# Causal attention with the negated maxima turned as 64 rows of one bank and placed by eight transfers, and another order at a layer's end

## The reference, cut to what matters

```python
scores = einsum('blhd,bmhd->bhlm', q, k) * scale
scores = where(causal, scores, -inf)
att = softmax(scores, axis=-1)
out = einsum('bhlm,bmhd->blhd', att, v)
return out.reshape(B, L, D) @ w_proj.T
```

```python
for i in range(6):
    x = attn_layer(shift_tokens(x), Wqkv[i], ...) + x
    x = ffn_layer(shift_tokens(x), ...) + x

def ffn_layer(x, ...):                 # per token
    xn = (x - mu) / sqrt(var + 1e-5) * g + bln
    a, gate = split(xn @ W1 + b1)
    return a * gelu(gate) @ W2 + b2
```

## Time and profile before

| | us |
|---|---|
| median of three runs | 5082.78 |
| lowest, highest | 5081.98, 5084.85 |
| the profiled execution, its own time | 5075.67 |
| its span | 5073.9 |
| TensorE matmuls busy | 4631.2 (91%) |
| weight loads busy (beside matmuls) | 2823.8 (56%) |
| VectorE, ScalarE, POOL busy | 3756.9, 2793.7, 2121.5 (74%, 55%, 42%) |

### The profile page before, as it was taken

How to read it: one execution, slowest core, us unless ns; L and a number is a source line. 1 busy time by engine, 2 the same in 40 slices (tenths; PEclk the granted TensorE clock), 3 DMA queues, 4 the chain that set the end, 5 groups by cost and what they waited for, 6 DMA issues and landing times. The chain is left out here.

```text
span 5073.9 us, 170071 instructions
## 1 busy us (share of the span) xinstructions
PE 4631.2 (91%) x75792; PEld 2823.8 (56%) x75792; DVE 3756.9 (74%) x4270; ACT 2793.7 (55%) x3791; POOL 2121.5 (42%) x1691
## 2 busy tenths in 40 slices
PE   7858887998788869999999999999999999999998
PEld 5623333444233346774767567655776567747674
DVE  5668883333788568886988589867897688868895
ACT  5527774223477745655656456555665556546564
POOL 4330000001000046654666366635665466546661
PEclk9979997999799989999999999999999999999999
DMA  0021111000111121111111111111111111111110
GB/s 23 12 69 33 43 44 35 0 0 27 59 40 41 30 63 40 40 36 45 41 41 39 41 40 42 38 44 40 40 40 53 30 38 41 38 43 40 40 40 26
DMA packets 95786, 192.97 MB, mean 38 GB/s; under 512 B 27088, under 2 KB 45520, under 8 KB 93264
## 3 DMA queue, kind: packets, MB, share of 16 engines
q1 hardware_dynamic: 95056, 182.09, 14.0%
HBM read 60.36 MB, written 15.73 MB: 15 GB/s over the span
## 5 line engine op out<-in xcount | busy, mean ns | idle before, releaser
L1854 POOL TENSOR_TENSOR part_of_layer<-part_of_layer,sine_of_layer 128x512 f32<-128x512 f32 x768 | 963.2, 1275 | 625.1 <-DVE sine_of_layer L1730 625.1
L1865 POOL TENSOR_TENSOR part_of_layer<-part_of_layer,inverse_of_layer 128x1024 f32<-128x1024 f32 x384 | 730.1, 1901 | 260.4 <-ACT inverse_of_layer L1613 245.4
L971 ACT ACTIVATE prob_of_ca<-ps 128x1024 f32<-128x1024 f32 (+3 forms) x768 | 591.6, 813 | 247.9 <-PE ps L845 175.9
L1727 DVE TENSOR_TENSOR part_of_layer<-ps,rope 128x1024 f32<-128x1024 f32 x384 | 466.1, 1214 | 39.1 <-ACT square_of_layer L1601 38.0
L1730 DVE TENSOR_TENSOR sine_of_layer<-ps,rope 128x1024 f32<-128x1024 f32 x384 | 465.1, 1211 | 0.0
L863 PE MATMUL ps<-keys_of_ca,queries_of_ca 64*128 64x512 bf16 (+3 forms) x1536 | 326.3, 342 | 137.3 <-DVE top_of_ca L1003 59.7
L1644 ACT ACTIVATE values_of_layer<-ps 128x1024 f32<-128x1024 f32 x192 | 196.5, 1024 | 456.2 <-PE ps L1494 456.2
L1513 PEld LDWEIGHTS ps<-prob_t_of_layer,mixed_of_layer 64*64 64x64 f32 x12288 | 340.8, 134 | 166.6 <-issue 157.7
L1520 PE MATMUL ps<-heads_out_of_layer,wo 128*128 128x128 f32 x3072 | 414.7, 279 | 15.0 <-ACT heads_out_of_layer L1633 14.1
L1766 DVE TENSOR_REDUCE total_of_layer<-prob_of_layer 128x16 f32<-128x1024 f32 x192 | 234.2, 1220 | 235.5 <-ACT prob_of_layer L1637 235.5
L1420 PE MATMUL ps<-qkv,shifted 128*128 128x512 f32 x768 | 384.2, 623 | 26.1 <-POOL values_of_layer L1868 20.5
(11 more groups left out here) (206 smaller groups left out, 9168.9 us busy)
## 6 DMA issues: line engine op xcount, KB each, us to landing
mixed_of_layer<-values_of_layer SPq DMA_DIRECT2D x636, 128.0 KB
mixed_of_layer<-values_of_layer SPq DMA_DIRECT2D x264, 64.0 KB
queries_of_ca<-q_parts SPq DMA_DIRECT2D x384, 32.0 KB
keys_of_ca<-k_parts SPq DMA_DIRECT2D x384, 32.0 KB
qkv<-in_qkv SPq DMA_DIRECT2D x6, 1536.0 KB, 6.7
q_parts<-parts_of_ci SPq DMA_DIRECT2D x16, 384.0 KB, 2.6
k_parts<-parts_of_ci SPq DMA_DIRECT2D x16, 384.0 KB, 2.6
rope<-in_rope SPq DMA_DIRECT2D x6, 1024.0 KB, 9.1
```

The lines of the kernel that those rows point to most:

```text
L971: nc.scalar.activation(prob[:, i % 2, 2 * two:2 * two + 2, j:], ps[:, 2 * two:2 * two + 2, j:], ACT.Exp, scale=scale).then_inc(raised, 1)
L1727: nc.vector.tensor_tensor(part[:, t % 2, side], by_head(slot), table(2 * side, t), ALU.mult).then_inc(parts, 1)
L1854: nc.gpsimd.tensor_tensor(out, out, sine[:, side, :, (1 - to) * half:(2 - to) * half], ALU.add).then_inc(rotated, 1)
L1865: nc.gpsimd.tensor_tensor(part[:, t % 2, side], part[:, t % 2, side], by, ALU.mult).then_inc(scaled, 1)
```

## The change

In the attention: the negated maxima are stored with the tile innermost, one product turns all 64 columns (4 heads, 2 parts, 8 tiles) into 64 rows of 128 in the lone bank, ScalarE copies 64 partitions of 128 elements, and each head and part is placed by a transfer of its own, from eight partitions of `rows` into one row of the stack: eight in place of four. The counting of the places by ScalarE and VectorE follows, and the two halves of the output product move from unit 9 to unit 10.

In the layers, at a layer's end: TensorE turns the last tile's probabilities ahead of the rest of the projection and of chunk 1's turn; it turns chunk 0 back right behind the last weighing, ahead of the last projection. ScalarE takes the first group's root a step earlier, writes chunk 0 ahead of the second group's square and root, and then loads GELU's table ahead of the copy of the last lower half. VectorE sums and evens chunk 0's squares ahead of centring chunk 1.

The whole diff, without the lines that follow from it in the counting:

```diff
-FINISH = {(0, 9): ("invert", 0), (1, 9): ("mix", 0), (2, 9): ("mix", 1)}
+FINISH = {(0, 9): ("invert", 0), (1, 10): ("mix", 0), (2, 10): ("mix", 1)}
+PLACES = 16 * 2 * HG
...
-        top, neg_parts = st.sb("top", [P, TOPS, HG]), st.sb("neg_parts", [P, TILES, HG, 2], BF16)
-        rows = st.sb("rows", [2 * HG, L], BF16)
+        top, neg_parts = st.sb("top", [P, TOPS, HG]), st.sb("neg_parts", [P, HG, 2, TILES], BF16)
+        rows = st.sb("rows", [2 * HG * TILES, P], BF16)
...
                     for h in range(HG):
                         row = ROW_HALF * (h % 2) + SHIFT_ROW
-                        sp.dma_start(stacks[G % RING_CA][0][row:row + 2, h // 2, :], rows[2 * h:2 * h + 2, :])\
-                            .then_inc(placed[G % RING_CA], 16)
+                        for part in range(2):
+                            to = stacks[G % RING_CA][0][row + part:row + part + 1, h // 2, :].rearrange("s (q n) -> s q n", n=P)
+                            first = (2 * h + part) * TILES
+                            sp.dma_start(to, rows[first:first + TILES, :]).then_inc(placed[G % RING_CA], 16)
...
                 def turn_rows(G):
-                    take_pair()
+                    take_lone()
                     pe.wait_ge(negated, 3 * (G + 1))
-                    for qt in range(TILES):
-                        last = nc.tensor.matmul(pair[0:2 * HG, qt // 4, qt % 4 * P:(qt % 4 + 1) * P],
-                                                neg_parts[:, qt].rearrange("p h s -> p (h s)"), k["ident_b"][:, :],
-                                                start=True, stop=True)
-                    last.then_inc(pair_ready, 1)
+                    nc.tensor.matmul(lone[0:2 * HG * TILES, 0:P], neg_parts[:].rearrange("p h s t -> p (h s t)"),
+                                     k["ident_b"][:, :], start=True, stop=True).then_inc(lone_ready, 1)
...
-                    nc.scalar.activation(rows[:, :], pair[0:2 * HG, :, :].rearrange("p a n -> p (a n)"),
-                                         ACT.Copy).then_inc(pair_used, 1)
+                    nc.scalar.activation(rows[:, :], lone[0:2 * HG * TILES, 0:P], ACT.Copy).then_inc(lone_used, 1)
...
-                    negate(nc.vector.tensor_scalar(neg_parts[:, :, :, 0], top[:, 0:TILES, :], -1.0, None, ALU.mult))
+                    negate(nc.vector.tensor_scalar(neg_parts[:, :, 0, :].rearrange("p h t -> p t h"), top[:, 0:TILES, :], -1.0, None, ALU.mult))
...
+                def turn_last_p(t):
+                    if t == NT - 1:
+                        turn_p(t)
+
+                def turn_other_p(t):
+                    if t < NT - 1:
+                        turn_p(t)
...
-                    steps((make_next_q, 0), (make_k, 0), (turn_q, 1), (project, 3), (last(lambda: turn(1)), 2), (turn_k, 1),
-                          (project_rest, 3), (turn_p, 2), (score, 1), (last(lambda: turn(0)), 1), (make_v, 0), (weigh, 2),
-                          (last(lambda: turn(2)), 2))
-                    back(0)
+                    steps((make_next_q, 0), (make_k, 0), (turn_q, 1), (project, 3), (turn_k, 1), (turn_last_p, 2),
+                          (project_rest, 3), (turn_other_p, 2), (last(lambda: turn(1)), 2), (score, 1), (last(lambda: turn(0)), 1), (make_v, 0), (weigh, 2),
+                          (last(lambda: turn(2)), 2), (last(lambda: back(0)), 2))
...
-                def first_invert():
-                    square_of(1)
-                    norm_invert(0)
...
-                    steps((square_next_q, 0), (square_k, 0), (out_q, 1), (out_k, 1), (out_p, 2), (last(first_invert), 2), (invert, 0),
-                          (out_v, 0), (raise_p, 1), (last(lambda: square_of(0)), 1), (out_o, 2), (shift_low, 4))
+                    steps((square_next_q, 0), (square_k, 0), (out_q, 1), (out_k, 1), (out_p, 2), (last(lambda: square_of(1)), 2), (invert, 0),
+                          (out_v, 0), (raise_p, 1), (last(lambda: square_of(0)), 1), (out_o, 2), (last(lambda: norm_invert(0)), 1), (shift_low, 4))
+                    reach(act, l, fetched, 16 * FETCHES)
+                    norm_out(0)
                     square_of(2)
                     norm_invert(1)
+                    nc.scalar.preload_act_table_set(GELU)
                     reach(act, l, added, NT)
                     low(NCH - 1, False)
-                    reach(act, l, fetched, 16 * FETCHES)
-                    norm_out(0)
...
                 def second_centre():
-                    centre(1)
                     spread_of(0)
                     norm_even(0)
+                    centre(1)
```

More of the change, by code:

```diff
@@ L52 @@
 LOG_AND_EXP = "natural_log_exp_and_others"
+GELU = "gelu_and_others"
 FIRST_SEM = 150
@@ L793, in _ @@
                 for slot in range(RING_CA):
-                    sp.wait_ge(placed[slot], 16 * HG * len(range(slot, ALL, RING_CA)))
+                    sp.wait_ge(placed[slot], PLACES * len(range(slot, ALL, RING_CA)))
             @block.gpsimd
@@ L894, in score @@
                     if i == 0 and two == 0:
-                        pe.wait_ge(placed[G % RING_CA], 16 * HG * (G // RING_CA + 1))
+                        pe.wait_ge(placed[G % RING_CA], PLACES * (G // RING_CA + 1))
                     if n >= 2:
@@ L944, in copy_rows @@
                 def copy_rows(G, n):
-                    act.wait_ge(pair_ready, n + 1)
+                    act.wait_ge(lone_ready, n + 1)
                     if G:
-                        act.wait_ge(placed[(G - 1) % RING_CA], 16 * HG * ((G - 1) // RING_CA + 1))
-                    nc.scalar.activation(rows[:, :], pair[0:2 * HG, :, :].rearrange("p a n -> p (a n)"),
-                                         ACT.Copy).then_inc(pair_used, 1)
-                    act.wait_ge(pair_used, n + 1)
+                        act.wait_ge(placed[(G - 1) % RING_CA], PLACES * ((G - 1) // RING_CA + 1))
+                    nc.scalar.activation(rows[:, :], lone[0:2 * HG * TILES, 0:P], ACT.Copy).then_inc(lone_used, 1)
+                    act.wait_ge(lone_used, n + 1)
                     act.sem_inc(rows_out, 1)
@@ L958, in sum_out @@
                                          ACT.Copy).then_inc(acc_out, 1)
[L960 to L963, removed]
+                alone = [pieces == 1 for _, pieces in MAXIMA]
+                lones = sum(alone) + alone[0]
+                copy_rows(0, lones)
+                lones += 1 + sum(alone[1:AHEAD])
                 for G in range(ALL):
@@ L973, in _ @@
                             if (i, two) == (ROWS_UNIT + 1, 0) and G + 1 < ALL:
-                                copy_rows(G + 1, pairs)
-                                pairs += 1
+                                copy_rows(G + 1, lones)
+                                lones += 1
+                            lones += (finishing(G, i, two) or ("",))[0] == "mix"
                             for m in maxima_at(G, i, two):
-                                pairs += in_pair[m % NM]
+                                lones += alone[m % NM]
                         if i == 4:
@@ L1015, in make_rows @@
                     negate(nc.vector.tensor_tensor(top[:, half:TILES, :], top[:, half:TILES, :], top[:, TILES:, :], ALU.max))
[L1016 to L1018 removed]
+                    negate(nc.vector.tensor_scalar(neg_parts[:, :, 0, :].rearrange("p h t -> p t h"), top[:, 0:TILES, :], -1.0, None, ALU.mult))
+                    negate(nc.vector.scalar_tensor_tensor(out=neg_parts[:, :, 1, :].rearrange("p h t -> p t h"),
+                                                          in0=top[:, 0:TILES, :], scalar=-1.0,
+                                                          in1=neg_parts[:, :, 0, :].rearrange("p h t -> p t h"), op0=ALU.mult, op1=ALU.subtract))
                 def invert(b):
@@ L1043, in between @@
                 def between(G, i, slot):
+                    if (i, slot) == (ROWS_UNIT + 1, 0) and G + 1 < ALL:
+                        next(lones)
                     if finishing(G, i, slot):
                         finish(G // GROUPS - 1, *finishing(G, i, slot))
-                    if (i, slot) == (ROWS_UNIT + 1, 0) and G + 1 < ALL:
-                        next(pairs)
                     for m in maxima_at(G, i, slot):
```

## The result

| | us |
|---|---|
| before, median of 4 runs beside the changed kernel | 5083.53 (5081.98 to 5084.85) |
| after, median of 4 runs | 5106.62 (5102.51 to 5117.09) |
| ratio, 95% interval | 1.0049 (1.0035 to 1.0063) |
| the profiled execution after, its own time and span | 5102.51, 5100.7 |

What follows compares the result with a forecast made beforehand. TensorE was taken to bound the kernel, idling for the rows' copy in attention and at three places per layer end. Attention +14.2 and layers -14.3 sum to -0.1 us, so 5082.7 us, range 5058 to 5106.

Steps and rivals of the forecast that it cites:

- (a) to (c): Attention turn: product about 0.1 us, copy 0.31 us, SyncE told at 508.35 not 509.04, next score could start 1.27 us earlier.
- (d): Attention rows: eight transfers issued 0.634 us apart delay the score 0.37 us per turn, 10.4 us over 28 turns.
- TensorE stood ready at 512.86: In the attention: TensorE could start the next group's first score at 512.86, though the rows land only at 514.50.
- the new wait costs the clock: Rival, attention: with issues at 0.70 us, a 2.1 us wait halves TensorE's clock; 5097 to 5122 us; chance 0.23.
- 14.2: Attention: microseconds added in total, 10.4 from 28 turns and 3.8 from the two last turns.
- (e): Attention: output product moved to unit 10 costs nothing under the wait, about 1 us in 10 turns if transfers were cheap.
- (f): Attention: SyncE busy with rows until 513.35, not 511.5; transfers of inverses and collection of sums behind them cost nothing.
- (g): Attention: VectorE's new layout for the negated rows and TensorE's turn waiting for the single bank cost nothing.
- Cheap transfers: Rival, attention: issues at 0.34 us, no score waits, attention -25.6 us, 5043 us in all; chance 0.2.
- The layers, -14.3: Six layer ends: third gate product 2.55 us earlier at the first, 2.35 at the other five, -14.3 us in all.

Runs made afterwards that it cites:

- four transfers: The changed kernel (after) with each head's 16 rows placed by one transfer, four in all in place of eight; ratio to before 0.9916.
- `norm_alone`: Before with the changed layer ends, except that the last tile's probabilities are turned where they were; ratio to before 0.9971.
- two transfers: The changed kernel (after) with the 64 rows laid so that two transfers of 32 rows place them all; ratio to before 0.9922.
- `layers_only`: The attention of before with the changed layer ends; ratio to before 0.9967.

## Why the prediction was wrong

It named the right place and the right two causes, and missed the size of one and the likelihood of the other. By its own steps:

- **(a) to (c), turn, copy, told SyncE.** Right: copy 0.26 us (0.31), first issue 1.15 us after the turn (1.20), the maxima's wait for the copy 0.29 us. The one turning product took 0.24 us and not 0.1; the copy waits for the exponential anyway, and nothing came of it.
- **(d) eight transfers at 0.634 us.** The failed step, a term mis-sized: from start to start it was 0.69. I had taken the distance of the old ones and kept 0.70 as the end of the range. Seven intervals make 0.39 us, and the score came 0.74 us later per turn in place of 0.37: 28 x 0.37 = 10.4 us. The landing, 1.73 us, was as predicted (1.71). The two last turns lost 2.3 us each in place of 1.9.
- **"TensorE stood ready at 512.86."** Right: that is 5.71 us after the turn, measured 5.61, and 5.60 with four transfers. So the wait grew by the issues alone: with 0.634 us each it was to be 1.64 us, with the measured 0.69 it was 2.04. That moved it from where the earlier trace rows had shown the clock to hold (1.65) to where the earlier trace rows had shown it to fall (2.07). The one row for "it holds" was thin: in `norm_alone` the same wait, at 1.78 us, did not hold.
- **The rival "the new wait costs the clock"**, with a chance of 0.23, is what happened, from the very point it had given: an issue near 0.70 us and a wait of 2.1 us. The sum had the clock at nothing. The rival put 18 falls at 1.4 us; there were ten, and without them the attention took 14.5 us less. With 14.2 + 10.4 + 0.8 + 14.5 = 39.9 us the +41.0 is accounted for but for 1.
- **(e) to (g).** (e) held under the wait: the groups with the output product took 28.65 us like the others. Without the wait it was to cost about 1 us and cost 1.64. (f) and (g) showed no cost of their own.
- **"Cheap transfers".** Wrong for this change: no issue was cheap. The kernels with two and four transfers came to its time by fewer issues, a ratio of 0.992, which on 5082.78 us is 5043 us, its number, but that is in part luck. It had 18 turns win 1.27 us, 10 with the output product win 0.27, and the last turns nothing. Measured: groups of 26.53 us (before 27.9) win 1.37, those of 28.17 lose 0.27, and the last turns win about 0.4 each.
- **The layers, -14.3.** Right: 14.6 in `layers_only`, 12.2 in the full change. The GELU came 2.5 us earlier at the first end, where I had 1.8, and the third gate product 3.2 in place of 2.55. About 1 us of both is luck of the clock: this end of before took 20.33 us, its five others 19.1 to 19.3, since its stretch at half clock was twice as long.

## What to carry to other kernels

A small transfer within SBUF held its queue for 0.5 to 0.7 us here, nearly the same for 2 KB as for 8. Ask for the layout that lets one transfer take the most rows, or share them between two queues, before shortening what feeds them; a stage that ends in eight issues is at least as long as eight issues. When a wait moves, work out its new length from both its ends, when the data come and when the engine is ready, because idle time can cost TensorE its clock as well (here waits of 2 us did in about half of the turns, and one of 1.78 us did; 1.65 us did not). What a freed engine gains is gone if the same edit sends it to wait for a queue.

## What the runs showed of the hardware

- The issue of a transfer from SBUF to SBUF took SyncE 0.56 us with 2 partitions of 1024 (before), 0.59 with one, 0.635 with 8 of 128, 0.61 with 16 and 0.63 with 32: nearly the same for 2 to 8 KB. Some 0.04 to 0.07 us lie between one issue and the next. On GpSimd's queue it took 0.518 us.
- A fall of the clock cost a group 1.1 to 1.2 us. In after, idle stretches of TensorE's matmuls of 1.97 us and more were followed by a fall in ten of eighteen turns; behind waits of 1.69 us or less at this place there was none, in after or with the old rows in eight. At another place 1.78 us (`norm_alone`) and 2.17 us (two transfers) were followed by a fall and 1.65 us (before) was not. A wait of 1.11 us came before a fall at four layer ends of `norm_alone`, at the one shown with 1.66 us idle shortly before; the same two waits in before had no second fall.
- Filling the wait with eight products that nobody needs is 16 us faster than leaving TensorE idle.
